# Cross-attention kernel: in the second batch of each group, the context loads and GpSimd's steps stand in another order

## The reference

```python
def _L0_xattn_ref(x, context, w_q, w_k, w_v, w_o, b_o):     # 16 heads of 64
    q = (x @ w_q).reshape(B, Sq, HEADS, DIM_HEAD).transpose(0, 2, 1, 3)
    k = (context @ w_k).reshape(...)
    v = (context @ w_v).reshape(...)
    sim = jnp.einsum('bhid,bhjd->bhij', q, k) * SCALE
    attn = jax.nn.softmax(sim, axis=-1)
    out = jnp.einsum('bhij,bhjd->bhid', attn, v)
    return out.transpose(0, 2, 1, 3).reshape(B, Sq, INNER) @ w_o + b_o

x = x + _L0_xattn_ref(_layernorm(x), ctx_768, ...)
x = x + _L0_attn_ref(_layernorm(x), ...)       # causal self-attention, 16 heads of 32
x = x + _L0_ffn_ref(_layernorm(x), ...)        # 512 -> 2048 -> 512, piecewise GELU
```

## Time and profile before

| | |
|---|---|
| median of 3 runs | 1712.68 us |
| profiled execution | 1714.3 us, its span 1712.4 us |
| TensorE matmul busy | 1623.2 us, 95% |
| VectorE busy | 1231.7 us, 72% |
| ScalarE busy | 1026.5 us, 60% |
| GpSimd busy | 796.5 us, 47% |
| granted TensorE clock, mean | 0.977 of full speed |

### The profile page before, as it was taken

How to read it: one execution, slowest core, us unless ns; L and a number is a source line. 1 busy time by engine, 2 the same in 40 slices (tenths; PEclk the granted TensorE clock), 3 DMA queues, 4 the chain that set the end, 5 groups by cost and what they waited for, 6 DMA issues and landing times. The chain is left out here.

```text
span 1712.4 us, 30263 instructions
## 1 busy us (share of the span) xinstructions
PE 1623.2 (95%) x11142; PEld 1402.6 (82%) x11142; DVE 1231.7 (72%) x2381; ACT 1026.5 (60%) x2036; POOL 796.5 (47%) x747
## 2 busy tenths in 40 slices
PE   6999999999999999999999999999986999999998
PEld 4878898888899888888889788989874777878786
DVE  5547878877787787877777684666655897867776
ACT  3337777767777676767776423444445665656554
POOL 3116546364563535545353231333434666454555
PEclk9999999999999999999999999999988899999999
DMA  8783434344343443423343861012112221010010
GB/s 265 210 234 94 125 93 109 114 107 131 83 124 90 116 124 90 138 76 110 113 131 86 276 214 64 27 50 75 63 51 81 86 74 56 19 50 19 19 38 25
DMA packets 173687, 173.38 MB, mean 101 GB/s; under 512 B 80930, under 2 KB 138338, under 8 KB 173540
## 3 DMA queue, kind: packets, MB, share of 16 engines
q1 hardware_dynamic: 173540, 171.45, 33.8%
HBM read 133.65 MB, written 37.75 MB: 100 GB/s over the span
## 5 line engine op out<-in xcount | busy, mean ns | idle before, releaser
L75 PE MATMUL p_bank_mix<-p_probt,p_ctx 128*128 128x512 f32 x1152 | 301.2, 407 | 22.1 <-issue 15.0
L75 PE MATMUL p_bank_score<-p_ctxt,p_qo 128*128 128x256 f32 x2304 | 304.6, 286 | 1.3 <-ACT p_probs L993 1.1
L75 PEld LDWEIGHTS p_bank_score<-p_ctxt,p_qo 128*128 128x128 f32 x2304 | 288.1, 191 | 6.5 <-issue 2.7
L75 PEld LDWEIGHTS p_bank_mix<-p_probt,p_ctx 128*128 128x128 f32 x1152 | 212.8, 194 | 66.3 <-issue 19.8
L1956 PE MATMUL p_bank_down<-p_w,p_ht 128*128 128x512 f32 x768 | 198.3, 405 | 1.8 <-DVE p_ht L2043 1.8
L1190 DVE SCALAR_TENSOR_TENSOR p_qo<-p_bank_mix,p_odd,p_qo 128x512 fp32r<-128x512 f32 x192 | 143.8, 749 | 60.1 <-ACT p_qo L1007 52.8
L1914 POOL TENSOR_TENSOR p_a<-p_a,p_g 128x512 f32<-128x512 f32 x64 | 112.0, 1751 | 160.8 <-ACT p_a L1994 160.8
L1956 PEld LDWEIGHTS p_bank_down<-p_w,p_ht 128*128 128x128 f32 x768 | 143.8, 191 | 40.0 <-issue 4.8
L1007 ACT ACTIVATE p_qo<-p_bank_mix,p_odd 128x512 fp32r<-128x512 f32 x192 | 132.3, 689 | 70.0 <-PE p_bank_mix L75 69.5
L706 POOL TENSOR_SCALAR p_probs<-p_probs,p_small 128x256 f32<-128x256 f32 x256 | 121.2, 480 | 102.4 <-DVE p_small L1177 102.0
L993 ACT ACTIVATE p_probs<-p_bank_score,p_small 128x257 f32<-128x257 f32 x256 | 121.2, 475 | 59.3 <-DVE p_small L1171 54.5
(11 more groups left out here) (276 smaller groups left out, 3687.0 us busy)
## 6 DMA issues: line engine op xcount, KB each, us to landing
p_blocks_in<-in_ctx_dram SPq DMA_DIRECT2D x256, 96.0 KB, 2.5
p_ctx_in<-in_ctx_dram SPq DMA_DIRECT2D x64, 384.0 KB, 3.2
q<-p_ctx SPq DMA_DIRECT2D x64, 256.0 KB, 3.4
p_odd_in<-in_ctx_dram SPq DMA_DIRECT2D x64, 192.0 KB, 3.5
p_x<-in_x_dram SPq DMA_DIRECT2D x32, 256.0 KB, 4.5
p_quad<-q SPq DMA_DIRECT2D x32, 256.0 KB, 3.3
p_probt<-q SPq DMA_DIRECT2D x32, 256.0 KB, 4.0
p_o_in<-o SPq DMA_DIRECT2D x8, 1024.0 KB, 7.6
```

Of the source, the lines that this page charges most:

```text
L75: made = e.matmul(out, lhsT, rhs, start=n == 0, stop=n == last)
```

## The change

The third batch's successor (in group 1: batch 11) has its two kinds of load issued in the second batch. In the second batch of each group `load_blocks` now stands ahead of `load_context` on SyncE. On GpSimd `low_context(b)` of the second batch stood between its second and third `scale`; now it is the first step of the batch, as it was already in all other batches.

```diff
                 for b in range(g * GB, (g + 1) * GB if g < NG else 0):
+                    if b % GB == 1:
+                        load_blocks(b + 2)
                     if b + 2 < B:
                         load_context(b + 2)
-                        if b % GB > 0:
+                        if b % GB > 1:
                             load_blocks(b + 2)
...
                 first, second = b % GB == 0, b % GB == 1
+                low_context(b)
                 for tile in range(NT):
-                    if tile == (2 if second else 0):
-                        low_context(b)
                     if tile == 2 and second:
                         shift(b + 1)
                     scale(b, tile)
```

## The result

The changed kernel takes 1701.82 us, the median of 9 runs (1698.8 to 1709.77). The kernel before took 1714.4 us in 9 runs on the same chips (1711.99 to 1716.6). The ratio is 0.9934, with a 95% interval of 0.9917 to 0.9951. So the change saves about 11 to 13 us, where I had forecast 20. The profiled execution took 1699.03 us with a span of 1697.1 us, at the fast end of its runs.

What follows compares the result with a forecast made beforehand. TensorE's pause at the third batch's mix, from late pieces, was taken as the bound. Excess goes from 32.7 to 11.2 us, 1.4 us given back: 1714.3 becomes 1694.2, or 1692.6 against the median 1712.68; range 1686 to 1703.

Steps and rivals of the forecast that it cites:

- TensorE's clock at its upper level: With at most 1.4 us of pause a group, TensorE's clock would stay up, except for one group allowed to fall.
- the 32.7 us of excess: Eight two-batch stretches, 181.87 us, exceed undisturbed pairs of 18.65 us; 21.5 us are mix pauses, the rest mostly slower matmuls.
- The pieces first on SyncE: Pieces issued 3.9 us earlier, so the third batch's mix loses its pause, 2.07 us in group 1, with 1.6 us cover.
- a help that costs nothing: `low_context(9)` first on GpSimd: `shift(10)` ends at 250.5 instead of 252.27; cost nothing, at most 0.5 us.
- `odd_in` after 4.1 us: `odd_in` of batch 11, issued behind pieces and `ctx_in`, usable 4.1 us later (3.56 to 5.57), so `shift(11)` starts at 255.2.
- 1.4 us of pause a group: The wait moves to the third batch's transposes by way of `odd_in` and GpSimd: 1.4 us a group, 0.9 to 2.9.
- 1.4 us given back for one group: Allowance of 1.4 us in the sum for one group whose TensorE clock falls all the same.
- my own signs of being wrong: The mix still waits, the clock falls in more than two groups, or `odd_in` takes 5 us.
- the wait comes back on GpSimd: Rival: `odd_in` takes 5 us or more, or the clock falls in most groups; about 1702 us (1698 to 1709); chance 0.22.
- The rule of the Trainium skill: DMA engines take descriptors in ring order, so `odd_in` cannot pass the pieces; 4.1 us taken instead of 3.56.

Runs made afterwards that it cites:

- e6: Changed kernel, but in every batch except a group's first, pieces precede context on SyncE and GpSimd's next shift stands between second and third scale; 1679.22 us.
- e2: Kernel before with only GpSimd's edit, `low_context` of the second batch first; SyncE's order as before; 1695.33 us, ratio 0.987.
- e8: Kernel before plus eight useless matmuls ahead of the mix that paused in each group's third batch; 1702.74 us, ratio 0.993.
- e4: Changed kernel plus 5 useless matmuls ahead of the first transposes of each group's third batch; 1687.77 us, ratio 0.9843.
- e1: Changed kernel with GpSimd's edit undone, so only the pieces stand first on SyncE; 1706.89 us, ratio 0.9953.
- e5: Changed kernel, but in the second batch SyncE issues `ctx_in`, then the pieces, then `odd_in`; 1689.24 us, ratio 0.9847.

## Why the prediction was off

The direction and the path of the wait were right, and the step that failed is the clock: I had TensorE's clock at its upper level in seven of eight groups, and it fell in four. The gain was 10.9 us against the median I started from, or 12.6 against the later one, and not 20.1.

- **What bounds the kernel, and the 32.7 us of excess.** Right, if a little small. The stretches of e6 are 181.87 - 146.76 = 35.1 us shorter, since an undisturbed pair takes 18.3 us there and not 18.65, and e6 comes out 36 us under the kernel before by the medians.
- **The pieces first on SyncE.** Right: the mix doesn't wait. In group 1 VectorE came to them 5.1 us after their first issue (reckoned 4.83) and didn't wait. But I took this edit for the source of the gain and GpSimd's for a help that costs nothing; e2 shows it the other way round.
- **`odd_in` after 4.1 us.** Its time from issue to use is 4.04 us on average, but the issue came 2.95 us after the start of `shift(10)` on average, not 2.5, since the four pieces took 1.8 to 3.1 us to issue, where I had the 1.91 of the kernel before. So `shift(11)` was 0.4 us later than reckoned, and scattered from 6.0 to 8.2.
- **1.4 us of pause a group.** The row has 12.6 us in 8 waits, 1.6 a group, against 11.2. That is a small miss in the mean. But I had it in two parts of 0.9 and 0.5 us with work between, and by my own sum that was wrong: the first `scale` ends at 259.3, so the first pair waits 1.2 of the 1.4. In the trace nearly all of it lies ahead of the first pair.
- **TensorE's clock at its upper level, because "in group 1 the clock held over 2.07", with 1.4 us given back for one group.** This is the step that failed. The clock fell in four of eight groups; the falls cost 5.8 us, and the slower work is 7.8 us in all, not 1.4. I had worked with the average pause of 1.4 us, while single ones were up to 2.72 us, and I had taken one row, of a group that held its clock over 2.07 us, as if it were a bound. The stretches before showed six groups that had lost it. Two of my own signs of being wrong came true: the clock fell in more than two groups, and `odd_in` took over 5 us in two.

So of the forecast 20 us, 10.3 were to come from the pauses and 9.8 from the clock. The trace has 9.1 and 2.7. The stretches add up to 170.06 us where I had said about 160; that the profiled time is only 5 us above the sum of 1694.2 is in part luck, since 3.5 us came from outside of them. e8 shows what the clock cost in the kernel before, 9.3 us, and e4 that in the changed kernel it no longer falls when the pause is filled. The rival "the wait comes back on GpSimd" (gain 4 to 16 us, by a slow `odd_in` or a clock that falls in most groups) is closer to what happened: two groups had the slow load, four the lower clock.

Two things I did not foresee. The pieces ahead of `odd_in` counted against the change more than I gave them: e2 keeps `odd_in` first and is 6 us faster by the medians, 11 by the ratios. In the way of `shift(11)` most of that is the later issue, 2.95 us after the start of `shift(10)` against 1.87 in e2, and little the landing, 4.04 us against 3.82. In six of the eight groups the landing took 3.3 to 4.1 us, 3.65 on average, so no longer than in e2; the mean is raised by the two of 5.04 and 5.35 us, and e4, with the same order of loads, has 3.91 with none above 4.49. The rule of the Trainium skill (page "DMA: Bandwidth & Descriptors", section "Queues, rings and completion order") has the completion carry the time of the loads ahead. These runs neither confirm it nor speak against it: I had given it 0.5 us, and a delay of that size is not to be seen in most groups. And the excess of a group is not the pause alone: over the eight groups 7.8 us of slower work came to 13.1 us of idle time.

## What to carry to other kernels

When a pause of TensorE is shortened, ask where each single pause ends up, not the average: those that stay long can still cost the clock, which here was about 1.45 us more for each of four pauses of 1.83 to 2.72 us. A wait that goes from one queue comes back at the next step queued ahead of its due time (pieces behind `odd_in`, scales behind `shift`), so give every step of every queue its due time and order the queue by it, as e6 does, before moving one load alone. To price the clock by itself, fill the pause with work whose result is thrown away.

## What the runs showed of the hardware

The granted clock held over some pauses and fell after others of the same length. In the changed kernel it held after 0.66, 0.87, 1.12 and 1.29 us and fell after 1.83, 2.00, 2.13 and 2.72 us. In e1 it fell after 1.79 us already. But it held after 1.79 and 1.84 us in e5, after 1.92 us in e2, and after 2.07 and 2.72 us in groups 1 and 2 of the kernel before. Group 2 there, TensorE's pause and its stretch:

```profile
360.48 1.63 PE L75 MATMUL p_bank_mix<-p_probt,p_ctx 128*128 128x512 f32 x6 [2.72 <-issue]
```

```profile
351.61:373.46 21.85, 18.78 (x124) 1.00 0.49 126
```

So the length of a pause alone doesn't tell, and what else decides is not shown here. In the 16 groups of e4 and e8, where matmuls filled the pause in whole or in part, the clock never fell.

The issue of the same four transfers of 96 KB took 1.91 or 1.92 us in all eight groups of the kernel before, but 1.93 us in group 1 and 3.12 us in group 2 of the changed kernel, and the queue behind was late by that much: `odd_in` went out 2.5 to 2.7 us after the start of `shift(10)` in four groups and 2.8 to 3.8 us in the others. No run here shows what slows it.
